# The shared feed-forward network of the first token group is moved into the first layer norm stage; the others follow as four and three groups

## The reference

```
x = x + 0.5 * ffn(layernorm(x))
x = x + attn(layernorm(x))      # W_in, a causal convolution of 4, a state recurrence of 16 states, silu, W_out
x = x + 0.5 * ffn(layernorm(x))

ffn(x):
    shared = (silu(x @ shared_gate.T) * (x @ shared_up.T)) @ shared_down.T
    logits = x @ gate_w.T                          # 8 experts
    top_id, score = argmax(logits), sigmoid(max(logits))
    routed = swiglu of expert top_id on x * score  # 8 experts, 256 -> 512 -> 256
    return shared + routed
```

## Time and profile before

| | |
|---|---|
| median of three runs | 959.91 us (958.92 to 960.01) |
| the profiled execution, its own time | 961.09 us |
| its span in the profile | 959.1 us |
| TensorE busy | 894.1 us, 93% of the span |
| VectorE, GpSimd, ScalarE busy | 50%, 48%, 40% |
| chain of work that ended last, by engine | PE 74%, DMA 11%, DVE 7%, issue 3%, POOL 2%, ACT 2% |
| mean granted TensorE clock | 0.986 of full |

### The profile page before, as it was taken

The page is one execution under the profiler, slowest core; times in us unless marked ns, Lnnn a source line. Parts: engine busy times, 40 slices in busy tenths (PEclk is TensorE's granted clock), DMA queues, the critical chain, the costliest instruction groups (busy, mean ns, idle before and its releaser), DMA issues.

```text
span 959.1 us, 16363 instructions
## 1 busy us (share of the span) xinstructions
PE 894.1 (93%) x5430; PEld 785.3 (82%) x5431; DVE 477.4 (50%) x1007; ACT 383.5 (40%) x747; POOL 460.8 (48%) x427
## 2 busy tenths in 40 slices
PE   3899998999999999996999997999899999998998
PEld 3787887888888878886989997888788888887887
DVE  6447553333333335556999984755333333333453
ACT  1134232333333433345677765423233333343331
POOL 3314764124242108856899885376431242220883
PEclk9999999999999999999999999799999999999999
DMA  8846464355555217511000103656434555511567
GB/s 277 285 126 230 159 241 162 114 187 180 180 186 183 92 46 146 70 26 23 1 23 24 45 23 121 203 175 233 180 117 180 186 180 180 187 55 50 95 100 185
DMA packets 75676, 130.85 MB, mean 136 GB/s; under 512 B 6650, under 2 KB 67716, under 8 KB 71268
## 3 DMA queue, kind: packets, MB, share of 16 engines
q0 software_dynamic: 18688, 74.33, 25.4%
q1 hardware_dynamic: 56932, 55.75, 18.3%
HBM read 93.74 MB, written 36.32 MB: 136 GB/s over the span
## 4 chain that ended last, share of the span: by engine, by line
PE 74%; DMA 11%; DVE 7%; issue 3%; POOL 2%; ACT 2%; SPq 1%; POOLq 0%; ACTq 0%; DVEq 0%
PE bank L350 20%; PE bank L352 19%; PE bank L351 19%; DMA rows<-xs_sorted 8%; PE bank L425 4%; PE bank L417 3%; PE bank L532 3%; PE bank L501 2%; DMA xs_sorted<-rows,pos 1%; DVE v L1164 1%; POOL xs_sorted L1438 1%; DMA rows<-xn_kept 1%; DVE xT_lo L945 1%; DVE stats L956 1%; DVE rows L1083 1%
## 5 line engine op out<-in xcount | busy, mean ns | idle before, releaser
L350 PE MATMUL bank<-wr_hi,xT_hi 128*128 x312 | 130.4, 418 | 9.9 <-issue 7.4
L1495 POOL DMA_INDIRECT acc<-ys_sorted,pos x64 | 102.4, 1600 | 74.6 <-DMA ys_sorted<-rows 41.0
L1471 POOL TENSOR_TENSOR wr_lo<-wr_raw,wr_hi 128x3072 fp32r<-128x3072 f32 x14 | 95.1, 6796 | 87.3 <-DMA wr_hi<-w_routed 87.3
L352 PE MATMUL bank<-wr_lo,xT_hi 128*128 x312 | 123.8, 397 | 0.0
L351 PE MATMUL bank<-wr_hi,xT_lo 128*128 x312 | 123.5, 396 | 0.0
L1121 DVE TENSOR_TENSOR hf<-sg,bank 128x512 f32<-128x512 f32 x78 | 53.7, 688 | 135.7 <-PE bank L352 135.7
L945 DVE TENSOR_TENSOR hT_lo<-bank,hT_hi 128x512 fp32r<-128x512 f32 x78 | 53.9, 692 | 125.6 <-ACT hT_hi L716 125.6
L350 PE MATMUL bank<-xT_hi,ws_hi 128*128 128x512 f32 x256 | 102.5, 400 | 3.9 <-DVE xT_lo L945 2.8
L716 ACT ACTIVATE xT_hi<-bank 128x256 fp32r<-128x256 f32 (+1 forms) x126 | 56.1, 463 | 117.0 <-PE bank L501 96.7
L351 PE MATMUL bank<-xT_hi,ws_lo 128*128 128x512 f32 x256 | 101.5, 396 | 0.0
L352 PE MATMUL bank<-xT_lo,ws_hi 128*128 128x512 f32 x256 | 101.3, 396 | 0.0
(11 more groups left out here) (236 smaller groups left out, 2257.5 us busy)
## 6 DMA issues: line engine op xcount, KB each, us to landing
wr_raw<-w_routed POOLq DMA_DIRECT2D x16, 1536.0 KB, 7.1
wr_hi<-w_routed POOLq DMA_DIRECT2D x16, 1536.0 KB, 7.8
rows<-xs_sorted SPq DMA_DIRECT2D x78, 128.0 KB, 2.5
ys_sorted<-rows SPq DMA_DIRECT2D x78, 128.0 KB, 1.7
xn_kept<-xg SPq DMA_DIRECT2D x16, 512.0 KB, 3.3
xg<-xn_kept SPq DMA_DIRECT2D x16, 512.0 KB, 4.3
rows<-xn_kept SPq DMA_DIRECT2D x16, 512.0 KB, 4.1
acc<-x SPq DMA_DIRECT2D x8, 512.0 KB, 7.5
```

The lines of the kernel that those rows point to most:

```text
L350: pe.matmul(o, a_hi, b_hi, start=start, stop=False, skip_group_check=True)
L352: return pe.matmul(o, a_hi, b_lo, start=False, stop=stop, skip_group_check=True)
L1471: pool.tensor_tensor(wr_lo[:, e % 2, :], wr_raw[:, :], f32(wr_hi[:, e % 2, :]), ALU.subtract).then_inc(s_wl, 1)
L1495: pool.indirect_dma_start(out=acc[:, tt, :], out_offset=None, in_=ys_dram, in_offset=bass.IndirectOffsetOnAxis(ap=pos[:, tt:tt + 1], axis= ...
```

## The change

The shared network of group 0 of layer 0 is done in the first layer norm stage. Its transposes are those that the logits of group 0 need anyway: ScalarE and VectorE cut them into high and low parts, and then ScalarE copies them for the logits. The four gate and up blocks stand one at a time between a group's transposes and its logits (after the transposes of groups 1 to 4), and the four down blocks follow. Groups 1 to 4 are then the first half and groups 5 to 7 the second. In layer 1 the halves stay groups 0 to 3 and 4 to 7.

For this several things move:

- The steps of `setup_ssm` are spread over the whole stage, and `setup_response`, `setup_rows` and `setup_toeplitz` go into the gate and up blocks of groups 1, 2 and 4 of the first half, in the PSUM banks 0 and 1. TensorE waits for what VectorE and ScalarE make of the first two before the transposes of groups 2 and 3.
- The small constants are loaded by ScalarE's queue instead of SyncE's, and `x` and the shared weights (in two parts) come first on SyncE's.
- GpSimd clears the identity before the other constants, starts the clearing of the sorted buffer one group sooner, and no longer waits for the end of the preparation before it starts to load expert 0.
- After the routed experts GpSimd gathers groups 0, 4, 1, 2 and 3, then group 5 when its shared part is added, then `ln2_rsqrt(0)` and `conv_bias(0)`, group 6, `ln2_rsqrt(1)`, group 7.
- The buffers of the preparation no longer lie under the experts' weights.

The diff, cut to its core:

```diff
-        def half_groups(half): return range(half * NH, (half + 1) * NH)
+        def half_groups(L, half):
+            if L == 0:
+                return range(1, NH + 1) if half == 0 else range(NH + 1, NG)
+            return range(half * NH, (half + 1) * NH)
...
             def shared(L, half):
...
+                    shared_gu(L, g, 0)
+                    shared_gu(L, g, 1)
+                    if L == 0 and g == 1:
+                        setup_response()
+                    if L == 0 and g == 2:
+                        setup_rows()
+                    if L == 0 and g == 4:
+                        setup_toeplitz()
+                    shared_gu(L, g, 2)
+                    shared_gu(L, g, 3)
+                    if L == 0 and g == 1:
+                        pe.wait_ge(s_rsv, 2)
+                    if L == 0 and g == 2:
+                        pe.wait_ge(s_fla, 1)
+                        pe.wait_ge(s_flv, 2)
...
-            for g in range(NG):
-                if g + 1 < NG:
-                    transposes((g + 1) % 2, s_xn, g + 2, 0, f_r1(g), XT1[(g + 1) % 2])
                 if g > 0:
                     pe.wait_ge(s_lgc, g)
-                logits(f_r1(g), LG1, xTf1[g % 2])
+                transposes(g % 2, s_xn, g + 1, min(g, 1), f_r1(g))
...
+            setup_ssm(4)
+            r1_transposes(1)
             pe.wait_ge(s_wsl, 1)
+            shared_gu(0, 0, 0)
+            setup_ssm(5)
+            r1_logits(1)
+            setup_ssm(6)
+            r1_transposes(2)
+            setup_ssm(7)
+            shared_gu(0, 0, 1)
+            r1_logits(2)
...
+            r1_transposes(5)
+            pe.wait_ge(s_wsl, 2)
+            pe.wait_ge(s_setv, 12)
+            shared_down(0, 0, 0)
+            r1_logits(5)
+            shared_down(0, 0, 1)
...
@@ VectorE @@
+                    if L == 0 and fb == 2 and g == 1:
+                        setup_response()
+                    if L == 0 and fb == 3 and g == 2:
+                        setup_rows_lo()
...
@@ GpSimd, after the routed experts @@
-            for g in half_groups(0):
+            gather(0, s_ga[0])
+            gather(NH, s_ga[NH])
+            for g in range(1, NH):
                 gather(g, s_ga[g])
-            for g in half_groups(1):
-                pool.wait_ge(s_add, 2 * (g + 1))
-                gather(g, s_ga[g])
-                if g == NH + 1:
+            for g in half_groups(0, 1):
+                if g == NH + 2:
                     ln2_rsqrt(0)
                     pool.wait_ge(s_step, 16)
                     conv_bias(0)
-                if g == NH + 2:
+                if g == NH + 3:
                     ln2_rsqrt(1)
+                pool.wait_ge(s_add, 2 * (g + 1))
+                gather(g, s_ga[g])
```

More of the change, by code:

```diff
@@ new lines, in shared_down @@
+            def shared_down(L, g, fb):
+                n = L * NG + g
+                pe.wait_ge(s_hl, 4 * n + fb + 1)
+                for t in range(GT):
+                    ts = slice(t * P, (t + 1) * P)
+                    cs = slice(DN0 + fb * H, DN0 + (fb + 1) * H)
+                    mm = mm3(pe, D2[t // 2][:, (t % 2) * H:(t % 2 + 1) * H], hT_hi[:, fb, ts],
+                             hT_lo[:, fb, ts], ws_hi[:, cs], ws_lo[:, cs],
+                             start=(fb == 0 and t % 2 == 0), stop=(fb == FB - 1))
+                    if fb == FB - 1 and t % 2 == 1:
+                        mm.then_inc(s_d, 1)
@@ L464, in shared @@
             def shared(L, half):
-                for g in half_groups(half):
-                    if g == half * NH:
+                groups = half_groups(L, half)
+                for g in groups:
+                    first, last = g == groups[0], g == groups[-1]
+                    if first:
                         if half == 0:
@@ L747, in shared @@
             def shared(L, half):
-                xt_hi(t_s(L, half * NH))
+                groups = half_groups(L, half)
+                xt_hi(t_s(L, groups[0]))
                 if half == 0:
@@ L759, in shared @@
                         ln2_hi(0)
-                    shared_group(L, g, t_s(L, g + 1) if g % NH < NH - 1 else None)
-                    if L == 0 and g == NH:
+                    shared_group(L, g, t_s(L, g + 1) if g != groups[-1] else None)
+                    if L == 0 and half == 1 and g == groups[0]:
                         cut_w_io()
@@ L1070, in shared_group @@
                     mix_lo(0)
[L1071 to L1075 removed]
+                add_shared(L, g)
             def scale_rows(L, g):
@@ L1088, in shared @@
                     choose(L)
-                xt_lo(c_s(L, half * NH))
+                groups = half_groups(L, half)
+                xt_lo(c_s(L, groups[0]))
                 if half == 0:
```

481 lines of the change are left out of this document (271 added, 210 removed).

## The result

The changed kernel takes 975.75 us (median of 4 runs, 971.52 to 977.61), the kernel before 959.96 beside it (958.92 to 961.34): a ratio of 1.0157, interval [1.0132, 1.0181]. It is slower by 15.8 us; the forecast was 6 us faster. The profiled execution took 976.43 us, with a span of 974.4 against 959.1.

The account below looks back on a forecast made before the run. TensorE was taken as the bound, busy 93% of the span, its first stage at the low clock. First stage -7.9, first half +5.4, second half -3.5 sum to -6.0 us: 954 us, forecast's own range 950.5 to 958, 8-in-10 range 946 to 963.

Parts of the forecast that it names:

- Small loads: Start of the first stage: small loads on ScalarE's queue beside x, cost taken as 0, bounds 0 and 2 us.
- First product at 22.0: First stage: the first gate and up product of 512 columns starts at 22.0 us.
- VectorE has `x` by then: Start of the first stage: SyncE issues x first, so VectorE has it when the doubling chain starts at 6.4 us.
- From there TensorE has a full row: First stage from 22.0 us: TensorE never waits, as VectorE needs about 4.8 us a group and TensorE at least 5.4.
- The clock lost about three times: First stage: clock rises in or just behind the first block, then is lost about three times, 1.7 us each, together 5.2.
- the stage's -7.9: First stage ends at 66.4 us instead of 74.34, so 7.9 us sooner.
- First half +5.4: First half: setup_response 1.8, setup_rows 2.1, wait before group 3 2.1, less a 0.6 stall; bounds +3 and +8 us.
- `setup_toeplitz` stands in the last group, where the pause of 4.0 us hides its 0.6: Last group of the first half: TensorE's 4.0 us pause covers setup_toeplitz; without that cover it would cost 0.6 us.
- Second half -3.5: Second half: group 7 waits about 12 us for ScalarE behind GpSimd's gathers, then low clock; gain 3.5 us, bounds 2 and 8.
- The rivals: Clock lost (0.17, 964 us), clock held (0.17, 949), GpSimd not holding group 7 (0.06, 940), VectorE ruling first stage (0.10, 959).
- Clock lost: Rival, chance 0.17: clock lost or never won between first-stage blocks; slower, 964 us taken, far end 977 with stage end 89.7.
- My bound for a wrong sign: First stage: an end of its last logits past 72 us would prove the forecast of a faster kernel wrong in sign.

Follow-up runs that it names:

- the two kernels with the mends together: Changed kernel with six fixes to its waits together, 0.9851 of the kernel before; the same with ln2_rsqrt(1) and the last zero store also moved earlier, 0.9823.

## Why the prediction was wrong, step by step

- **Small loads, taken as 0 with bounds 0 and 2:** 1.64 us at the first product. A term of the first stage mis-sized, within its bounds. The doubling chain itself, which I had "at 6.4 us as before", started at 9.34, outside them.
- **First product at 22.0:** 25.37. Half of the difference is the small loads. The run with these loads back on SyncE shows where the other 1.7 us are: 1.0 because the statistics wait for `x` until 7.44 and not 6.4 ("VectorE has `x` by then" failed), and 0.6 in the steps from there to the transposes, which took 5.1 us for 4.5. From the transposes to the product it took 11.2 us for 11.1.
- **"From there TensorE has a full row":** failed. I set VectorE's work against TensorE's and left out what else VectorE waits for: `norm_apply(4)` writes where the rows of group 2 are kept from, and that store took 13.12 us behind the zeros (the run with spread zeros). Gap 3.46 us, and the clock low from 41.1 to 47.9.
- **The clock lost about three times, the stage's own length:** right. It fell three times. From the first product to the last logits I had 44.4 us; it took 47.8 with the gap. In the two kernels with the mends together it took 44.4 and 41.6, and the logits end at 68.20 and 65.26, on either side of the forecast of 66.4. So the stage's -7.9 was about what was there to be had, but behind two waits on DMAs: measured -1.2 at the last logits, -1.4 at the first half.
- **First half +5.4:** +17.4. This is the largest part of the loss. `setup_response` (1.9), `setup_rows` (2.1) and the wait before group 3 (2.17 where nothing holds `qq`) were as costed. What failed is "`setup_toeplitz` stands in the last group, where the pause of 4.0 us hides its 0.6". That pause covers TensorE's work; it does not cover VectorE's work ahead of the down products. There `tt_lo` and the three instructions of `setup_b_out`, to which I gave no cost at all, now stand ahead of the last two `hT_lo`, and one instruction of this row meets GpSimd's cut of expert 1: `bo_t`, the copy behind it, or an `hT_lo`. In the kernel before, the last `hT_lo` ends at 147.24 and the cut starts at 147.31: the two miss each other by 0.07 us, and I had not looked. With the hold and the clock behind it this is 8.8 us, and the bounds of +3 to +8 did not hold it. The held `qq` and its clock are another 2.9. 5.4, 8.8 and 2.9 give 17.1 of the 17.4. That the cut of GpSimd is the cause is shown (the run in which the cut waits); that `tt_lo` alone would do is read from the run without the bias instructions.
- **Second half -3.5:** -2.6, with the gap (10.77 for 12 us), its cause and the low clock behind it (5.9 us for 4.3) as forecast. The gathers take 1.91 us each on average in the earlier trace rows (23 steps in 43.83 us), not the 1.85 that I read. Right in mechanism, and shown by moving `ln2_rsqrt(0)` alone.
- **The rivals:** none is what happened. "Clock lost" had the sign but not the place; the clock was lost as often as in the forecast itself. Its far end, 977, is near the measured time by chance: it has the stage end at 89.7, and that end came at 73.14. My bound for a wrong sign, a stage end past 72, was met by this, though most of the loss lies behind the stage.

Of the 21.3 us between the forecast's -6.0 and the +15.3 of the spans, 6.5 stand in the first stage (-7.9 against -1.4), 12.0 in the first half, 0.9 in the second half and 1.9 in the routed slots and the rest.

## What to carry to other kernels

An instruction's duration belongs to its place: when a change moves work on VectorE, list what GpSimd runs at the new time, and look for two SBUF inputs or an SBUF-to-SBUF copy beside a long elementwise instruction of GpSimd. A wait of 1.5 us on the engine with slack was worth 8.8 us here. When a stage loses a group, look for what was hidden by it (the order of GpSimd's gathers), and mend that with the change: the same order was free before. And ask of every buffer that is written again who must have read it, transfers among them.

## What the runs showed that was not expected

- One row of 256 is held as long as a full tile: 7.59 instead of 0.41 us beside the cut of 6.7 us, 4.12 instead of 0.27 for a copy. The time stands in the instruction's own length, with no wait shown.
- It seems to work both ways, by the traces alone, since no run took VectorE's instructions away: GpSimd's scatter took 2.49 instead of 1.16 us, and its 128x4 `ve<-mv` of the first stage takes 0.23 us or up to 1.97 beside VectorE, as in GpSimd's timeline of the changed kernel:

```profile
53.54 1.97 POOL L1462 TENSOR_SCALAR ve<-mv 128x4 f32<-128x4 f32 x1 [4.28 <-DVE mv L1044]
```

- A 512 KB store landed 13.12 us after its issue behind 4.9 MB of stores from another queue, where the median of the 16 such stores is 4.1 us. With those stores spread, the wait for it was gone.
